# Attention with three slots a step instead of five, and the output projection gathered at the end of each round

## The chip, the cores and the metric

The kernel runs on one core of a Trainium2 chip. Its engines run side by side, each with its own queue of instructions in program order: TensorE (PE in the profile, its weight loads PEld), VectorE (DVE), ScalarE (ACT), GpSimd (POOL) and SyncE (SP), which issues most DMAs. They wait for one another on semaphores. TensorE writes its results into PSUM, eight banks of 128 partitions by 512 f32 numbers, from where VectorE and ScalarE read them. The metric is the device time of one execution in microseconds.

## What is computed

The program is a transformer block with two layers' parts: multi-query attention and a quantised feed-forward product, then a mixture of experts, a second attention and a second mixture of experts. The change is in the first attention alone: 2 batches, 1024 rows, 16 heads of 64 channels, one key and value head shared by all, a causal mask, and one extra "null" key.

```python
q = (xn @ Wq).reshape(b, n, H, DH).transpose(0, 2, 1, 3) * scale
k, v = (kv[..., :DH], kv[..., DH:])
...
sim = jnp.einsum('bhid,bjd->bhij', q, k)
sim = sim + bias
...
attn = jax.nn.softmax(sim, axis=-1)
out = jnp.einsum('bhij,bjd->bhid', attn, v)
out = out.transpose(0, 2, 1, 3).reshape(b, n, INNER)
out = out @ Wo
```

## The kernel before

The 1024 rows of a batch are 8 tiles of 128, and under the mask tile t sees t + 1 blocks of 128 keys. A **round** j, b pairs the long row tile 7 - j with the short row tile j of batch b, so that every round has 9 blocks. There are 8 rounds (j = 0 to 3, two batches each), and a round has 8 **steps**, one for each pair of heads; 64 steps in all. In the code unit 0 is the long row, unit 1 the short one.

A step's work comes in two streams. The **score stream** works for a later step: TensorE makes one of six chunks of scores (long row, head 0, two chunks; long row, head 1, two chunks; short row, one chunk a head; called s0 to s5 here), VectorE adds the bias, stores it in `probs` and keeps the minimum (L2265), ScalarE takes the exponential when a row and head is complete (L2200), VectorE inverts the sum (L2305), GpSimd multiplies the long row by it (L2154) and ScalarE the short one (L2210). Once a step TensorE also makes the queries of four steps later ("q", L2347), which ScalarE and VectorE split into a high and a low part (L2194, L2272). Chunks and queries share a **ring of two banks**, `s_ps`: item e goes to bank e % 2, and TensorE waits until item e - 2 has been read, by `wait(pe, s_read, e - 1)`. SyncE loads the bias and moves the queries.

The **value stream** works for the present step. It is cut into slots of up to two key blocks, five a step. `turn(n)` on TensorE transposes the probabilities of slot n into a bank `t_ps` (L2369), `high(n)` on ScalarE copies them rounded to `pT_hi` (L2182), `low(n)` on VectorE takes the rest to `pT_lo` (L2287), and `weigh(n)` on TensorE multiplies both parts with the values into `o_ps` (L2389, L2390). There are three `t_ps` banks. When a row ends, ScalarE copies the lower half of `o_ps` (L2187), VectorE adds the two halves into `oT` (L2300), and `project` multiplies it with `Wo` into the bank `y_ps`, which gathers the whole round (L2398). At the end of a round the null key's share is added (L2403), and ScalarE copies the result to `yacc` (L2216).

The order on each engine is written out by hand. Step x occupies slots 5x to 5x + 4, and the table `SCORES_AT` says at which slot a score chunk or query stands: of step x + 2 the chunks s0 and s1 in the first slot, then one chunk a slot, and the query in the third. At slot n TensorE does the first score item, a projection if a row ended three slots ago, `turn(n + 2)`, the other score items, `weigh(n)`. ScalarE does `high(n + 1)`, the copy of a row that ended, the query, the exponentials. VectorE does the first score item, `low(n + 1)`, the other items, the sum of a row that ended, the inversion.

## Time and profile before

| | |
|---|---|
| median of 3 runs | 1084.52 us (1079.64 to 1092.77) |
| span of the profiled execution | 1077.8 us |
| attention, from the first to the last transposition into `t_ps` | 60.8 to 610.1 us |
| busy over the span: TensorE, VectorE, ScalarE, GpSimd | 86%, 74%, 68%, 57% |
| granted TensorE clock in the attention, between 100 and 600 us | 1.00 |

The profile is of one execution on one core, taken by the hardware. Its own time is not in the table of runs; the span is from its first instruction to its last, 6.7 us below the median. A row of the timeline gives start and duration in us, then engine, line, operation, output and inputs, shape, and how many instructions were merged; in brackets the idle time before it and what ended that. Matmuls are pipelined, so a row's duration is longer than the distance to the next matmul: four transpositions have the duration 0.60 us and follow one another every 0.11 us.

### The profile page before, as it was taken

The page shows a single profiled execution, that of the slowest core. Times are in us where ns is not written, and L with a number is a line of the kernel's source. Part 1 is how long each engine was busy: PE and PEld are TensorE (multiplying, and loading weights), DVE is VectorE, ACT ScalarE, POOL GpSimd, SP SyncE. Part 2 cuts the span into 40 slices and gives each one's busy share as a digit, 9 for nine tenths or more (in the row PEclk, how much of TensorE's full clock was granted, in tenths as well). Part 3 has the DMA queues.
Part 4 walks back from the last instruction along what each step waited for, and adds up shares of the span by engine and source line. Part 5 has one row for each costly group of instructions (what it writes and reads, how often), then busy time and mean ns, then how long its engine had stood idle before and what let it go on. Part 6 is the DMA issues. An engine that isn't in the chain of part 4 may idle for free. (4 is left out here: it accounts for less than half of the span.)

```text
span 1077.8 us, 22664 instructions
## 1 busy us (share of the span) xinstructions
PE 930.0 (86%) x6178; PEld 811.2 (75%) x6178; DVE 799.7 (74%) x2315; ACT 735.9 (68%) x1651; POOL 610.6 (57%) x745
## 2 busy tenths in 40 slices
PE   7899999999999999999999849678753882499996
PEld 5578888888888998988888637568752662399995
DVE  7579989899898998988888798465458776244443
ACT  2278888888888998989989656235564552466663
POOL 2368878777676676755555364544572147244444
PEclk8889999999999999999999969799976885699998
DMA  9166666667566666665666031348926013444453
GB/s 308 38 184 182 177 179 181 177 175 199 156 189 198 179 190 179 192 205 165 192 175 199 28 133 42 115 147 270 320 86 196 21 69 133 107 77 78 76 82 45
DMA packets 110549, 162.83 MB, mean 151 GB/s; under 512 B 15993, under 2 KB 84089, under 8 KB 109402
## 3 DMA queue, kind: packets, MB, share of 16 engines
q1 hardware_dynamic: 99272, 142.16, 44.6%
q0 software_dynamic: 10560, 19.18, 7.8%
q8 instruction: 54, 0.88, 0.3%
q14 instruction: 69, 0.57, 0.2%
q10 hardware_dynamic: 594, 0.04, 0.0%
HBM read 110.63 MB, written 25.53 MB: 126 GB/s over the span
## 5 line engine op out<-in xcount | busy, mean ns | idle before, releaser
L2154 POOL TENSOR_SCALAR probs<-probs,inv_sum 128x1024 f32<-128x1024 f32 (+3 forms) x128 | 301.4, 2368 | 172.9 <-DVE inv_sum L2305 172.9
L2287 DVE TENSOR_TENSOR pT_lo<-t_ps,pT_hi 128x512 fp32r<-128x512 f32 (+1 forms) x320 | 202.8, 634 | 21.1 <-ACT pT_hi L2182 20.6
L2200 ACT ACTIVATE probs<-probs,neg_max 128x1025 f32<-128x1025 f32 (+7 forms) x256 | 197.6, 772 | 29.9 <-DVE neg_max L2265 28.6
L2369 PE MATMUL t_ps<-ident,probs 128*128 128x128 f32 x1152 | 180.3, 275 | 1.1 <-DVE pT_lo L2287 1.1
L2182 ACT ACTIVATE pT_hi<-t_ps 128x512 fp32r<-128x512 f32 (+1 forms) x320 | 175.3, 549 | 6.4 <-PE t_ps L2369 3.2
L2389 PE MATMUL o_ps<-pT_hi,values 128*128 128x256 f32 x576 | 174.8, 323 | 5.3 <-DVE pT_lo L2287 3.5
L2265 DVE CUSTOM_DVE_ANT_0 probs<-s_ps,bias_set,neg_null 128x512 f32<-128x512 f32 (+3 forms) x256 | 164.3, 642 | 4.5 <-PE s_ps L2338 2.8
L2369 PEld LDWEIGHTS t_ps<-ident,probs 128*128 128x128 f32 x1152 | 142.2, 141 | 31.3 <-DVE pT_lo L2287 3.1
L2390 PE MATMUL o_ps<-pT_lo,values 128*128 128x256 f32 x576 | 150.2, 280 | 0.0
L2337 PE MATMUL s_ps<-k_hi,q_hilo 128*128 128x512 f32 (+3 forms) x384 | 143.1, 373 | 4.7 <-DVE neg_max L2265 1.5
L2338 PE MATMUL s_ps<-k_lo,q_one 128*128 128x512 f32 (+3 forms) x384 | 134.4, 350 | 0.0
L2389 PEld LDWEIGHTS o_ps<-pT_hi,values 128*128 128x128 f32 x576 | 108.8, 189 | 16.8 <-issue 8.3
L1772 POOL DMA_INDIRECT out_dram<-yacc,xs x39 | 63.4, 1626 | 89.8 <-DVE yacc L1841 51.1
L2390 PEld LDWEIGHTS o_ps<-pT_lo,values 128*128 128x128 f32 x576 | 109.6, 190 | 0.0
L153 POOL DMA_INDIRECT routed_rows<-rt_rows,rt_rows_at x64 | 68.0, 1062 | 49.8 <-DVE rt_rows_at L198 31.3
L2337 PEld LDWEIGHTS s_ps<-k_hi,q_hilo 128*128 128x128 f32 x384 | 73.2, 191 | 16.6 <-DVE part_max L2265 10.1
L2398 PE MATMUL y_ps<-wo,oT 128*128 128x256 f32 x256 | 77.0, 382 | 0.5 <-DVE oT L2300 0.4
L2338 PEld LDWEIGHTS s_ps<-k_lo,q_one 128*128 128x128 f32 x384 | 73.6, 192 | 0.0
L2300 DVE TENSOR_TENSOR oT<-o_ps,o_low 64x128 f32<-64x128 f32 x256 | 71.4, 279 | 2.3 <-ACT o_low L2187 0.6
L1785 ACT ACTIVATE w_qkv<-m_x_ps,ln_b,ln_w 128x128 f32<-128x128 f32 x78 | 31.4, 454 | 59.7 <-PE m_x_ps L1855 59.7
L2265 DVE CUSTOM_DVE_ANT_0 probs<-s_ps,bias_set,part_max 128x512 f32<-128x512 f32 (+3 forms) x128 | 69.7, 545 | 1.5 <-PE s_ps L2338 1.3
L2347 PE MATMUL s_ps<-xs,wq_all 128*128 128x128 f32 x496 | 67.7, 280 | 2.9 <-DVE neg_max L2265 2.9
(348 smaller groups left out, 2135.3 us busy)
## 6 DMA issues: line engine op xcount, KB each, us to landing
bias_set<-bias_dram SPq DMA_DIRECT2D x16, 1024.0 KB, 5.4
bias_set<-bias_dram SPq DMA_DIRECT2D x16, 896.0 KB, 5.4
bias_set<-bias_dram SPq DMA_DIRECT2D x16, 768.0 KB, 4.9
bias_set<-bias_dram SPq DMA_DIRECT2D x16, 640.0 KB, 4.7
q_hilo<-q_hi SPq DMA_DIRECT2D x128, 64.0 KB, 2.0
q_hilo<-q_lo SPq DMA_DIRECT2D x128, 64.0 KB, 2.0
q_one<-q_hi SPq DMA_DIRECT2D x128, 64.0 KB, 2.0
bias_set<-bias_dram SPq DMA_DIRECT2D x16, 512.0 KB, 5.5
```

The costliest lines, as they stand in the source:

```text
L2154: last = pool.tensor_scalar(keys, keys, inv_sum[:, x.set, unit, h:h + 1], None, ALU.mult)
L2182: act.activation(pT_hi[n % 3][:, 0:count, :], t_ps[TURNS["slot", n] % 3][:, 0:2 * P * count], ACT.Copy).then_inc(hi_out, 1)
L2200: act.activation(p, p, ACT.Exp, scale=-1.0, bias=neg_max[:, x.set, row.unit, h:h + 1], accum_out=row_sum[:, x.set, row.unit, h:h + 1]).the ...
L2265: dve.tensor_tensor_reduce(probs_row(x, row, h)[:, 1 + P * first:1 + P * (first + count)], s_ps[e % 2][:, 0:P * count], bias_row(x, row, h ...
L2287: dve.tensor_tensor(pT_lo[n % 3][:, 0:count, :], t_ps[TURNS["slot", n] % 3][:, 0:2 * P * count].rearrange("p (n q) -> p n q", n=count), pT ...
L2300: last = dve.tensor_tensor(oT[row.unit][DH * h:DH * h + DH, :], o_ps[row.unit][0:DH, cols], o_low[row.unit][:, cols], ALU.add)
L2337: pe.matmul(s_ps[e % 2][:, 0:P * count], q_hilo[x.set][h][:, mine], k_hi[:, cols], start=True, stop=False)
L2338: pe.matmul(s_ps[e % 2][:, 0:P * count], q_one[x.set][h][:, mine], k_lo[:, cols], start=False, stop=True).then_inc(s_ready, 1)
L2369: last = pe.transpose(t_ps[at % 3][:, P * (2 * m + h):P * (2 * m + h) + P], probs_row(x, row, h)[:, 1 + P * (k + m):1 + P * (k + m) + P], ...
L2389: pe.matmul(o_ps[row.unit], v, pT_hi[n % 3][:, m, :], start=(k + m == 0), stop=False)
L2390: last = pe.matmul(o_ps[row.unit], v, pT_lo[n % 3][:, m, :], start=False, stop=(k + m == row.blocks - 1))
L2398: pe.matmul(y_ps[:, row.unit, :], oT[row.unit][:], wo[:, x.pair, :], start=first, stop=False, skip_group_check=True).then_inc(projected, 1)
```

## The change

Slots are up to four blocks instead of two, and a step has three: two for the long row (half of it each) and one for the short row. The two `t_ps` buffers are two PSUM banks each. The bank for them comes from `y_ps`, which goes. `oT` keeps the outputs of all eight pairs of a round, and the projection becomes an item of the score ring: at the round's end, for each of the two rows, eight products and the null key's one are made in a row into an `s_ps` bank ("y"), and ScalarE copies it. The transposed null weights go through the ring as well ("null").

The order by hand changes with it. Each slot has two chunks of scores: s2 and s3 in a step's first slot, s4 and s5 in its second, and s0 and s1 of the next step in its third. The query is third in the first slot in rounds j = 0 and 1, and third in the second slot in rounds j = 2 and 3. TensorE does `turn(n + 1)` (before: `turn(n + 2)`), then all score items of the slot, then `weigh(n)`.

```diff
-SLOTS_A_STEP = 5
+SLOTS_A_STEP = 3
...
-        self.slots = [(k, min(2, self.blocks - k)) for k in range(0, self.blocks, 2)]
+        half = self.blocks if unit else (self.blocks + 1) // 2
+        self.slots = [(k, min(half, self.blocks - k)) for k in range(0, self.blocks, half)]
...
-SCORES_AT = {n: [] for n in range(-1, NS)}
+SCORES_AT = {n: [] for n in range(-1, NS + 3)}
 for _x in range(STEPS):
-    for _i, _t in enumerate((0, 0, 1, 2, 3, 4)):
+    for _i, _t in enumerate((-1, -1, 0, 0, 1, 1)):
         SCORES_AT[max(-1, SLOTS_A_STEP * (_x - LEAD) + _t)].append(("s", _x, _i))
     if _x >= FIRST_Q:
-        SCORES_AT[max(-1, SLOTS_A_STEP * (_x - QLEAD) + 2)].append(("q", _x))
+        _at = SLOTS_A_STEP * (_x - QLEAD)
+        SCORES_AT[max(-1, _at + (ROUNDS[max(0, _x - QLEAD) // PAIRS][0] >= 2))].append(("q", _x))
+    if (_x + 1) % PAIRS == 0:
+        _r, _end = _x // PAIRS, SLOTS_A_STEP * (_x + 1)
+        SCORES_AT[_end - 1].append(("null", _r))
+        SCORES_AT[_end].append(("y", _r, 0))
+        SCORES_AT[_end + 1].append(("y", _r, 1))
 SCORES_AT[-1].sort(key=lambda item: (item[1] - (QLEAD - LEAD - 0.5 if item[0] == "q" else 0), item[0], item[2:]))
-RING = {item: i for i, item in enumerate(item for n in range(-1, NS) for item in SCORES_AT[n])}
+for _n in range(NS + 3):
+    SCORES_AT[_n].sort(key=lambda item: ("null", "s", "q", "y").index(item[0]))
+ORDER = [item for n in range(-1, NS + 3) for item in SCORES_AT[n]]
+RING = {item: i for i, item in enumerate(ORDER)}
...
-        self.pT_hi = [sbuf(st, f"pT_hi{i}", [P, 2, 2 * P], F32R) for i in range(3)]
-        self.pT_lo = [sbuf(st, f"pT_lo{i}", [P, 2, 2 * P], F32R) for i in range(3)]
-        self.oT = [sbuf(st, f"oT{i}", [P, P]) for i in range(2)]
+        self.pT_hi = [sbuf(st, f"pT_hi{i}", [P, 4, 2 * P], F32R) for i in range(2)]
+        self.pT_lo = [sbuf(st, f"pT_lo{i}", [P, 4, 2 * P], F32R) for i in range(2)]
+        self.oT = [sbuf(st, f"oT{i}", [P, PAIRS, P]) for i in range(2)]
...
-        t_ps = [psum(st, f"t_ps{i}", [P, CW]) for i in range(3)]
+        t_ps = [psum(st, f"t_ps{i}", [P, 4 * 2 * P]) for i in range(2)]
         o_ps = [psum(st, f"o_ps{i}", [P, CW])[:, 0:2 * P] for i in range(2)]
-        y_ps = psum(st, "y_ps", [P, 2, D])
...
-                    wait(act, pv_done, n - 2)
+                    wait(act, pv_done, n - 1)
                     act.wait_ge(turn_ready, n + 1)
-                    act.activation(pT_hi[n % 3][:, 0:count, :], t_ps[TURNS["slot", n] % 3][:, 0:2 * P * count], ACT.Copy).then_inc(hi_out, 1)
+                    act.activation(pT_hi[n % 2][:, 0:count, :], t_ps[n % 2][:, 0:2 * P * count], ACT.Copy).then_inc(hi_out, 1)
...
-                def result(r):
+                def result(r, unit):
                     j, b = ROUNDS[r]
-                    act.wait_ge(y_ready, r + 1)
-                    for unit, tile in enumerate((QT - 1 - j, j)):
-                        last = act.activation(yacc[:, QT * b + tile, :], y_ps[:, unit, :], ACT.Copy)
-                    last.then_inc(y_out, 1)
+                    e = RING["y", r, unit]
+                    act.wait_ge(s_ready, e + 1)
+                    apart(act, marks_act)
+                    act.wait_ge(s_read, e)
+                    act.activation(yacc[:, QT * b + (j if unit else QT - 1 - j), :], s_ps[e % 2][:, 0:D], ACT.Copy).then_inc(s_read, 1)
...
+                def null_weights(r):
+                    e = RING["null", r]
+                    dve.wait_ge(s_ready, e + 1)
+                    dve.tensor_copy(null_wT[r % 2][:], s_ps[e % 2][0:H, 0:2 * P]).then_inc(s_read, 1)
+
                 def fill(item):
+                    e = RING[item]
+                    if e and ORDER[e - 1][0] == "y":
+                        dve.wait_ge(s_read, e)
                     if item[0] == "q":
                         query(item[1])
-                    else:
+                    elif item[0] == "s":
                         scores(item[1], item[2])
+                    elif item[0] == "null":
+                        null_weights(item[1])
...
+                def project(r, unit):
+                    e = RING["y", r, unit]
+                    pe.wait_ge(oT_ready, units_done(PAIRS * r + PAIRS - 1, unit))
+                    pe.wait_ge(s_read, RING["null", r] + 1)
+                    wait(pe, s_read, e - 1)
+                    for pair in range(PAIRS):
+                        pe.matmul(s_ps[e % 2][:, 0:D], oT[unit][:, pair, :], wo[:, pair, :], start=(pair == 0), stop=False)
+                    pe.matmul(s_ps[e % 2][:, 0:D], null_wT[r % 2][:, P * unit:P * unit + P], null_wo[:],
+                              start=False, stop=True).then_inc(s_ready, 1)
...
-                def project(x, row):
-                    first = x.pair == 0 and row.unit == 0
-                    if first:
-                        wait(pe, y_out, x.round)
-                    pe.wait_ge(oT_ready, units_done(x.g, row.unit))
-                    pe.matmul(y_ps[:, row.unit, :], oT[row.unit][:], wo[:, x.pair, :],
-                              start=first, stop=False, skip_group_check=True).then_inc(projected, 1)
-                    if x.pair == PAIRS - 1 and row.unit == 1:
-                        pe.wait_ge(t_read, TURNS["null", x.round] + 1)
-                        for unit in range(2):
-                            last = pe.matmul(y_ps[:, unit, :], null_wT[x.round % 2][:, P * unit:P * unit + P], null_wo[:],
-                                             start=False, stop=True, skip_group_check=True)
-                        last.then_inc(y_ready, 1)
 
                 for item in SCORES_AT[-1]:
                     fill(item)
-                for n in range(2):
-                    turn(n)
-                for n in range(NS + 6):
-                    if n < NS:
-                        for item in SCORES_AT[n][:1]:
-                            fill(item)
-                    ended = ends_at(n - 3)
-                    if ended:
-                        project(*ended)
-                    if n < NS:
-                        turn(n + 2)
-                    if n < NS:
-                        for item in SCORES_AT[n][1:]:
-                            fill(item)
-                    if n < NS:
-                        weigh(n)
+                turn(0)
+                for n in range(NS + 3):
+                    turn(n + 1)
+                    for item in SCORES_AT[n]:
+                        fill(item)
+                    weigh(n)
```

On TensorE, in a step of a round with j = 1 (7 and 2 blocks), before: from the second product of s2 (128x512) over a projection, a turn, a `weigh` and s3 (128x384) to the query, which is the last row.

```order
L2338 MATMUL s_ps<-k_lo,q_one_1 128x512
L2398 MATMUL y_ps<-wo,oT 128x256
L2369 MATMUL t_ps<-ident,probs 128x128 x2
L2389 MATMUL o_ps<-pT_hi,values 128x256
L2390 MATMUL o_ps<-pT_lo,values 128x256
L2389 MATMUL o_ps<-pT_hi,values 128x256
L2390 MATMUL o_ps<-pT_lo,values 128x256
L2337 MATMUL s_ps<-k_hi,q_hilo_1 128x384
L2338 MATMUL s_ps<-k_lo,q_one_1 128x384
L2398 MATMUL y_ps<-wo,oT 128x256
L2369 MATMUL t_ps<-ident,probs 128x128 x4
L2347 MATMUL s_ps<-xs,wq_all 128x128 x4
```

After, the same place: s2, s3 and the query stand in a row.

```order
L2396 MATMUL t_ps<-ident,probs 128x128 x6
L2343 MATMUL s_ps<-k_hi,q_hilo_1 128x512
L2344 MATMUL s_ps<-k_lo,q_one_1 128x512
L2343 MATMUL s_ps<-k_hi,q_hilo_1 128x384
L2344 MATMUL s_ps<-k_lo,q_one_1 128x384
L2353 MATMUL s_ps<-xs,wq_all 128x128 x4
L2410 MATMUL o_ps<-pT_hi,values 128x256
L2411 MATMUL o_ps<-pT_lo,values 128x256
```

The query is two ring items behind s2 in both. Now only s3 stands between them, where before a projection, two turns and a `weigh` did as well.

On VectorE before the change, from the read of s2 to the query's split. `L2265` is the read of a score chunk, its second row the accumulator's.

```order
L2265 ISA probs,part_max<-s_ps,bias_set,neg_null 128x512
L2265 ISA part_max 128x1
L2287 TENSOR_TENSOR pT_lo<-t_ps,pT_hi 128x512
L2265 ISA probs,neg_max<-s_ps,bias_set,part_max 128x384
L2265 ISA neg_max 128x1
L2287 TENSOR_TENSOR pT_lo<-t_ps,pT_hi 128x256
L2272 SCALAR_TENSOR_TENSOR q_lo<-s_ps,q_hi 128x256
```

After, from the low part of a step's first slot (1024 columns) over the read of s2 (the second chunk of 128x512, part_max) to the query's split and what stands behind it:

```order
L2296 TENSOR_TENSOR pT_lo<-t_ps,pT_hi 128x1024
L2264 ISA probs,neg_max<-s_ps,bias_set,part_max 128x384
L2264 ISA neg_max 128x1
L2306 TENSOR_TENSOR oT<-o_ps,o_low 64x128 x2
L2311 RECIPROCAL inv_sum<-row_sum 128x2
L2264 ISA probs,part_max<-s_ps,bias_set,neg_null 128x512
L2264 ISA part_max 128x1
L2296 TENSOR_TENSOR pT_lo<-t_ps,pT_hi 128x768
L2264 ISA probs,neg_max<-s_ps,bias_set,part_max 128x384
L2264 ISA neg_max 128x1
L2271 SCALAR_TENSOR_TENSOR q_lo<-s_ps,q_hi 128x256
L2306 TENSOR_TENSOR oT<-o_ps,o_low 64x128 x2
```

The read of s2 now stands behind a low part of twice the columns, the read of s1, the long row's sum and an inversion.

On ScalarE, from the copy of a query to the high part of the next step's first slot (its last `pT_hi` row), in a round with j = 1, before:

```order
L2194 ACTIVATE q_hi<-s_ps 128x256
L2182 ACTIVATE pT_hi<-t_ps 128x512
L2200 ACTIVATE probs,row_sum<-probs,neg_max 128x897
L2182 ACTIVATE pT_hi<-t_ps 128x512
L2187 ACTIVATE o_low<-o_ps 64x256
```

And after:

```order
L2194 ACTIVATE q_hi<-s_ps 128x256
L2200 ACTIVATE probs,row_sum<-probs,neg_max 128x897
L2182 ACTIVATE pT_hi<-t_ps 128x512
L2200 ACTIVATE probs,row_sum<-probs,neg_max 128x897
L2210 ACTIVATE probs<-probs,inv_sum 128x256 x2
L2182 ACTIVATE pT_hi<-t_ps 128x1024
```

Two exponentials and the short row's two products with the inverse now lie between the query's copy and that high part, where one exponential did.

Behind a round's end on TensorE after the change (the first step of round 4, `SCORES_AT` slot 3 * 32 + 1): the projection of round 3's short row, between the slot's score items and its `weigh`.

```order
L2343 MATMUL s_ps1<-k_hi,q_hilo1_1 128x384
L2344 MATMUL s_ps1<-k_lo,q_one1_1 128x384
L2353 MATMUL s_ps0<-xs,wq_all 128x128 x4
L2372 MATMUL s_ps1<-wo,oT1 128x256 x8
L2373 MATMUL s_ps1<-null_wo,null_wT1 128x256
```

Before, these eight products were spread over the eight steps, one a step and row, as the first piece of this section shows.

## Rows read from the trace of the kernel before

**Rows 1.** The page: busy time, share of the span and instructions of each engine.

```profile
PE 930.0 (86%) x6178; PEld 811.2 (75%) x6178; DVE 799.7 (74%) x2315; ACT 735.9 (68%) x1651; POOL 610.6 (57%) x745
```

**Rows 2.** Windows: stretch, length, busy us of each engine, granted clock, DMA.

```profile
300.00:400.00 100.00, 98.88 (x714) 89.54 (x713) 91.36 (x284) 90.71 (x215) 70.23 (x96) 1.00 0.63 185
...
720.00:1078.00 358.00, 265.92 (x1741) 235.69 (x1739) 188.41 (x447) 185.76 (x385) 158.77 (x157) 0.85 0.47 122
```

**Rows 3.** Waits from 70 to 600 us: who for whom, total us, times, longest.

```profile
ACT q_hi L2194 <- PE s_ps L2347: 34.5, 47, 1.9
DVE q_lo L2272 <- ACT q_hi L2194: 23.3, 38, 1.8
...
PEld s_ps L2337 <- DVE part_max L2265: 7.8, 31, 0.3
```

**Rows 4.** Timeline, one step of round 2 (j = 1), TensorE.

```profile
302.02 0.19 PEld L2337 LDWEIGHTS s_ps<-k_hi,q_hilo 128*128 128x128 f32 x1 [0.24 <-DVE part_max L2265]
...
303.71 0.34 PE L2337 MATMUL s_ps<-k_hi,q_hilo 128*128 128x384 f32 x1
...
304.06 0.59 PE L2398 MATMUL y_ps<-wo,oT 128*128 128x256 f32 x2
...
304.49 0.60 PE L2369 MATMUL t_ps<-ident,probs 128*128 128x128 f32 x4
...
304.93 1.06 PE L2347 MATMUL s_ps<-xs,wq_all 128*128 128x128 f32 x8
...
305.74 0.36 PE L2389 MATMUL o_ps<-pT_hi,values 128*128 128x256 f32 x1
...
306.30 0.28 PE L2337 MATMUL s_ps<-k_hi,q_hilo 128*128 128x256 f32 x1
...
310.59 0.19 PEld L2337 LDWEIGHTS s_ps<-k_hi,q_hilo 128*128 128x128 f32 x1 [0.24 <-DVE part_max L2265]
```

**Rows 5.** Timeline, the same step, ScalarE.

```profile
302.33 0.60 ACT L2182 ACTIVATE pT_hi<-t_ps 128x512 fp32r<-128x512 f32 x1
...
303.20 1.05 ACT L2200 ACTIVATE probs<-probs,neg_max 128x897 f32<-128x897 f32 x1 [0.27 <-DVE neg_max L2265]
...
304.24 0.89 ACT L2210 ACTIVATE probs<-probs,inv_sum 128x256 f32<-128x256 f32 x2
...
305.04 0.36 ACT L2182 ACTIVATE pT_hi<-t_ps 128x256 fp32r<-128x256 f32 x1
...
306.08 0.39 ACT L2194 ACTIVATE q_hi<-s_ps 128x256 fp32r<-128x256 f32 x1 [0.68 <-PE s_ps L2347]
```

**Rows 6.** Timeline, the same step, VectorE.

```profile
303.02 0.57 DVE L2300 TENSOR_TENSOR oT<-o_ps,o_low 64x128 f32<-64x128 f32 x2
...
303.71 0.73 DVE L2265 CUSTOM_DVE_ANT_0 probs<-s_ps,bias_set,neg_null 128x512 f32<-128x512 f32 x1
...
304.37 0.69 DVE L2287 TENSOR_TENSOR pT_lo<-t_ps,pT_hi 128x512 fp32r<-128x512 f32 x1
...
304.97 0.61 DVE L2265 CUSTOM_DVE_ANT_0 probs<-s_ps,bias_set,part_max 128x384 f32<-128x384 f32 x1
...
305.50 0.42 DVE L2287 TENSOR_TENSOR pT_lo<-t_ps,pT_hi 128x256 fp32r<-128x256 f32 x1
...
306.50 0.42 DVE L2272 SCALAR_TENSOR_TENSOR q_lo<-s_ps,q_hi 128x256 fp32r<-128x256 f32 x1 [0.58 <-ACT q_hi L2194]
```

**Rows 7.** Timeline, VectorE: the same query split in five rounds, marks for a round's length.

```profile
138.90 0.42 DVE L2272 SCALAR_TENSOR_TENSOR q_lo<-s_ps,q_hi 128x256 fp32r<-128x256 f32 x1 [1.36 <-ACT q_hi L2194]
...
209.19 0.42 DVE L2272 SCALAR_TENSOR_TENSOR q_lo<-s_ps,q_hi 128x256 fp32r<-128x256 f32 x1 [1.79 <-ACT q_hi L2194]
...
351.41 0.42 DVE L2272 SCALAR_TENSOR_TENSOR q_lo<-s_ps,q_hi 128x256 fp32r<-128x256 f32 x1 [1.29 <-ACT q_hi L2194]
...
485.56 0.42 DVE L2272 SCALAR_TENSOR_TENSOR q_lo<-s_ps,q_hi 128x256 fp32r<-128x256 f32 x1 [1.09 <-ACT q_hi L2194]
...
555.99 0.42 DVE L2272 SCALAR_TENSOR_TENSOR q_lo<-s_ps,q_hi 128x256 fp32r<-128x256 f32 x1 [1.08 <-ACT q_hi L2194]
```

75 lines of the change are left out of this document (34 added, 41 removed).

## The prediction

> **What bounds the kernel now.** I read the page first, for the size of the part that changes. Then I read the windows of the attention, the table of waits, and the timeline of one step. The page [rows 1] has TensorE at 86% of the span and VectorE at 74%. That is a mean over stages, and the change touches only the attention, some 550 of 1078 us. In a window inside it [rows 2] TensorE is busy 98.9 of 100 us, and VectorE and ScalarE 91 each, at a granted clock of 1.00. By that view TensorE is the limit. The timeline says less than that: the busy rows overlap. The distances between rows are the work: transpositions 0.11 us each (four from 304.49 to 304.93), a query (304.93 to 305.74) and a chunk of 384 columns 0.35 us (303.71 to 304.06), so one of 512 is 0.47 and one of 256 (a little over the share) 0.24, a projection product 0.43 (304.06 to 304.49), a weighing product 0.12 (four in the 0.56 us from 305.74 to 306.30, with some wait in front) [rows 4]. The query's eight instructions take 0.92 at that spacing. A step has 18 transpositions, 18 weighing products, six chunks, a query and two projection products: 2.0 + 2.1 + 2.1 + 0.9 + 0.9 = 8.0 us. The step itself takes 302.02 to 310.59, 8.57 us [rows 4], so TensorE is at 93%, and the missing 0.6 us is in the waits.
>
> The waits name a loop over three engines [rows 3]: ScalarE waits for the query (34.5 us in all), VectorE for ScalarE's copy of it (23.3 us), TensorE for VectorE's read of a chunk, in order to get its ring bank back (7.8 us). It can be followed through one step: the bank is free at 302.02, TensorE works until the query, ScalarE copies it at 306.08, VectorE splits it at 306.50 and then works without a gap through s4, a low part, s5, a low part, the sum and s0, whose end frees the bank at 310.59 [rows 4 to 6]. So the period is 4.06 us on TensorE and its hand-over, 0.42 us on ScalarE and 4.09 us on VectorE. The kernel is held by this loop, not by an engine's load, and the question for the change is what its loop will be.
>
> **The change: what it removes.** Slots fall from 320 to 192, so 128 copies on ScalarE and 128 subtractions on VectorE go. A copy of 512 columns takes 0.60 us and one of 256 takes 0.36 [rows 5], so 0.12 of it is fixed; a subtraction takes 0.69 and 0.42 [rows 6], fixed 0.15. Two a step are 0.24 us on ScalarE and 0.30 on VectorE, 15 and 19 us over 64 steps if either were the limit. A copy of 1024 columns should be 1.08 us and a subtraction 1.23 (both worked out from those two rows; no instruction over two banks is in the trace, and I keep 0.1 us either way). TensorE's work stays at 8.0 us a step in the mean. GpSimd, SyncE and the DMAs keep their order per step and have slack (GpSimd busy 70 of 100 us [rows 2]); I cost them at nothing, and their inputs come no later against their use.
>
> **What it adds: a longer loop.** In rounds j = 0 and 1 the query is third in its slot, behind s2 and s3, and needs the bank of s2. Before, TensorE came to it long after that read. Now only s3 is between. VectorE reads s2 behind the low part of the first slot, s1, the sum and the inversion. That low part needs ScalarE's high part, and ScalarE does that behind the query's copy, two exponentials and the short row's products. So for j = 1, from the end of one read of s2:
> TensorE takes up the query in 0.2 us (an estimate, from the hand-over at 302.02), and ScalarE starts its copy 1.15 us later (304.93 to 306.08) [rows 4, 5]: 1.35.
> ScalarE in a row: the query 0.39, exponential 1.04 (303.20 to 304.24), high part of two blocks 0.60, exponential 1.04, short row's products 0.80 (304.24 to 305.04), high part of four blocks 1.08 [rows 5]: 4.95, or 4.85 since successive starts lie closer.
> VectorE in a row: low part of four blocks 1.15 (start to start), read of s1 0.53 (304.97 to 305.50), sum 0.60 (before 303.71), inversion 0.1, read of s2 0.73 [rows 6]: 3.1.
> Together 9.3 us, against 8.57. The side paths are shorter: TensorE goes from the query through weigh, turn, s4, s5, weigh and turn to s0 in 4.8 us and is early by 0.4 us. The same additions for the other rounds (exponentials and reads scaled by their columns) give 9.15 us for j = 0. For j = 2 and 3, where the query is third in the second slot and needs the bank of s4, two low parts and both sums are on the way, and they give 9.6 and 9.4.
>
> **What it adds: the projection in a row.** Eight products and the null key's are nine times 0.43, 3.9 us, in each of two neighbouring slots. Queued behind them on TensorE is weigh, and behind that the turn and the chunks for which ScalarE and VectorE wait. Their queues hold some 1 to 2 us of work by then and then run dry. The first product also waits for the read of the chunk two before it, 0.2 to 0.6 us. In the loop above, both lie between the query and the next high part, so I add them nearly whole: 4.35 + 4.3 us for j = 1, after taking off the 0.4 us that TensorE is early; 9.1, 8.6, 8.0 and 8.8 us for j = 0 to 3. The bounds are 2 us (all but the excess over the other engines' queues hidden) and 9 us. I take the upper part, for the nearest case in the trace: two j = 1 rounds take 351.41 - 209.19 = 142.2 us [rows 7], 71.1 each, and eight steps of 8.57 are 68.6. The null products, their copy and the two result copies, some 1 us of TensorE, cost 2.5 us of time. What stands at a round's end is not hidden in this pipeline. The null copy now comes ahead of the low part and s0: 0.7 us a round.
>
> **The sum.** Round lengths before are 70.3 us (j = 0), 71.1, 67.1 (half of 485.56 - 351.41) and 70.4 (j = 3) [rows 7]; they hold the projection and the round's end. After: 8 x 9.15 + 9.1 = 82.3, 8 x 9.3 + 8.6 = 83.0, 8 x 9.6 + 8.0 = 84.8, 8 x 9.4 + 8.8 = 84.0. The differences are 12.0, 11.9, 17.7 and 13.6 us, twice each: 110 us. The null copies add 5. The last two steps have no scores, and the last projection of the long row hides in part: less 5. That is 110 us on a profiled span of 1077.8, and the same on the median: 1084.5 + 110 = **1195 us**, 10% slower.
>
> The Trainium skill ("Perfetto Trace Analysis", Matmul Optimizations) says that it is important that matmuls run back to back in batches, because the engine's power follows its use. That speaks for the gathered projection; but the granted clock is 1.00 here already [rows 2], so by this trace the batch has nothing to win. The same page (Matmuls) wants independent groups to rotate through banks, so that the reading of one overlaps the next: three groups in a row on a ring of two do less of that.
>
> **The rivals.**
> *Faster: the ring holds nobody.* If VectorE comes to s2 before TensorE comes to the query, the engines' loads decide. TensorE's 8.0 us a step against 8.57 saves 0.57 x 64 = 36 us, and the exposed last projection gives 4 back: 1052 us. For it: fewer instructions, fewer waits. It decides once ScalarE's chain from the query to the high part is 3.5 us instead of 4.85 (9.3 less 1.3 is TensorE's 8.0); above 4.1 us the steps are slower than before. Against it: the orders as printed, and rows 5. 7%.
> *One half only.* The steps lengthen (for j = 0 to 3 by 0.6, 0.7, 1.6 and 0.9 us, 16 steps each) and the batches hide: 61 us, 1145. Or the batches cost and the steps stay as they are: 110 less 61 is 49 us, 1134. For them: both are walks through queues, and a queue that runs ahead further than I let it hides one or the other. 20%.
> *The clock falls.* TensorE will wait some 2 us in each step and more around the batches. In the last third of the program, where it is busy 266 of 358 us, its granted clock is 0.85 [rows 2]. At 0.85 the query and the batches in the loop, 2.2 us a step, are 18% longer: 25 us more, 1220; if its side chain becomes the longer one, 1240. The Trainium skill ("TensorE: Matmul & The Clock Gate", What's actually happening) has throttled as the default, which activity releases. 12%.
> *No change*, gains and losses of the same size: 5%.
> The forecast itself has 56%.
>
> **How the numbers follow.** The likeliest case is 1195. To hold 8 in 10, the range goes down to the half cases, 1135 and up to the clock's, 1235. Within 1% is about what a measurement of this kernel can't tell from no change. Faster by more than that 0.07, within it 0.05, slower 0.88.
>
> **What would show it.** In the profile after: the same query splits 9.1 to 9.6 us apart in a round's middle; TensorE's idle time or long first matmul in front of the query, released by VectorE's read; ScalarE without a gap from q_hi to the copy of 1024 columns; a row of 16 or 18 projection matmuls of 3.9 us, with VectorE idle behind it; rounds of 82 to 85 us. It is wrong if the query doesn't wait for VectorE, if ScalarE's or VectorE's two-bank instructions are much shorter than by the slopes, or if VectorE stays busy through a projection.

## The result, and the profile after

The changed kernel takes 1231.39 us (median of 4 runs, 1228.48 to 1236.10), the kernel before 1084.47 us beside it: a ratio of 1.1343 [1.1291, 1.1394], 147 us more. The profiled execution has a span of 1226.7 us and a mean granted clock of 0.910 (before 1077.8 us and 0.921). The forecast was 1195 us in a range of 1135 to 1235.

The page of the changed kernel: the span, the busy time of each engine (before in [rows 1]), the granted clock in 40 slices, and two groups of the attention.

```profile
span 1226.7 us, 22188 instructions
...
PE 982.4 (80%) x6178; PEld 833.6 (68%) x6178; DVE 794.8 (65%) x2187; ACT 723.8 (59%) x1523; POOL 614.8 (50%) x745
...
PEclk8899999988988999999999999697899598589999
...
L2182 ACT ACTIVATE pT_hi<-t_ps 128x768 fp32r<-128x768 f32 (+3 forms) x192 | 155.1, 808 | 38.4 <-PE t_ps L2396 35.6
...
L2194 ACT ACTIVATE q_hi<-s_ps 128x256 fp32r<-128x256 f32 x62 | 23.9, 385 | 123.9 <-PE s_ps L2353 123.9
```

The removed instructions are gone (128 fewer on VectorE, 128 fewer on ScalarE), and both engines are busy for less time than before. Neither was the limit. ScalarE now idles 123.9 us in front of the 62 copies of a query: two microseconds in each step.

The windows of the changed kernel, columns as in [rows 2]: one in j = 1, one in j = 3.

```profile
300.00:400.00 100.00, 84.78 (x519) 74.31 (x518) 66.32 (x192) 63.69 (x141) 55.40 (x72) 0.90 0.49 141
500.00:600.00 100.00, 85.47 (x541) 69.33 (x540) 69.80 (x199) 67.52 (x145) 48.66 (x73) 1.00 0.48 141
```

TensorE fell from 98.9 busy us of 100 to 85, and VectorE and ScalarE from 91 to between 64 and 70. The first window also shows a granted clock of 0.90, where it was 1.00 before. In both windows no engine is full; that is a loop's picture, and the waits name it (70 to 700 us, columns as in [rows 3]).

```profile
DVE probs L2264 <- PE s_ps L2344: 132.7, 82, 7.0
ACT q_hi L2194 <- PE s_ps L2353: 116.9, 57, 2.8
PEld s_ps L2343 <- DVE neg_max L2264: 68.5, 71, 1.4
PEld s_ps L2353 <- DVE part_max L2264: 32.5, 31, 1.1
```

The last row is the wait of the forecast: TensorE holds the query back until VectorE has read s2. ScalarE waited 34.5 us for the query before [rows 3], now 116.9. The first row has the round's end in it: 7.0 us at the longest, for a chunk that stands behind a projection.

A step of the changed kernel in j = 0, as a timeline of TensorE, ScalarE and VectorE.

```profile
182.62 1.16 PE L2353 MATMUL s_ps<-xs,wq_all 128*128 128x128 f32 x8 [0.61 <-DVE part_max L2264]
...
183.88 0.39 ACT L2194 ACTIVATE q_hi<-s_ps 128x256 fp32r<-128x256 f32 x1 [2.23 <-PE s_ps L2353]
184.16 1.14 ACT L2200 ACTIVATE probs<-probs,neg_max 128x1025 f32<-128x1025 f32 x1
185.29 0.37 ACT L2182 ACTIVATE pT_hi<-t_ps 128x256 fp32r<-128x256 f32 x1
185.56 1.15 ACT L2200 ACTIVATE probs<-probs,neg_max 128x1025 f32<-128x1025 f32 x1
186.69 0.69 ACT L2210 ACTIVATE probs<-probs,inv_sum 128x128 f32<-128x128 f32 x2
187.32 1.03 ACT L2182 ACTIVATE pT_hi<-t_ps 128x1024 fp32r<-128x1024 f32 x1
...
187.99 0.75 DVE L2264 CUSTOM_DVE_ANT_0 probs<-s_ps,bias_set,neg_null 128x512 f32<-128x512 f32 x1 [1.00 <-PE s_ps L2344]
188.67 1.22 DVE L2296 TENSOR_TENSOR pT_lo<-t_ps,pT_hi 128x1024 fp32r<-128x1024 f32 x1
189.81 0.74 DVE L2264 CUSTOM_DVE_ANT_0 probs<-s_ps,bias_set,part_max 128x512 f32<-128x512 f32 x1
...
191.96 1.16 PE L2353 MATMUL s_ps<-xs,wq_all 128*128 128x128 f32 x8 [0.61 <-DVE part_max L2264]
```

From query to query it is 191.96 - 182.62 = 9.34 us. ScalarE goes from the query's copy to the copy of 1024 columns without a gap. Here a second branch of the loop is as long: VectorE idles 1.00 us until TensorE has s0 ready at 187.99, and only then comes to the low part. ScalarE's copy of 1024 columns is done at 188.35 (187.32 + 1.03), the low part starts at 188.67: by these rows it is s0, and not ScalarE's chain, that makes the step 9.33 where the walk had 9.15. The two-bank instructions take 1.03 and 1.22 us, against 1.08 and 1.23 by the slopes.

The batch of the long row behind the last round of j = 2 (it stands in the first step of j = 3), in the same three engines:

```profile
589.10 3.69 PE L2372 MATMUL s_ps<-wo,oT 128*128 128x256 f32 x16 [1.00 <-DVE part_max L2264]
592.72 0.69 PE L2373 MATMUL s_ps<-null_wo,null_wT 16*128 16x256 f32 x2
593.35 0.38 PE L2410 MATMUL o_ps<-pT_hi,values 128*128 128x256 f32 x1
...
593.54 0.39 ACT L2218 ACTIVATE yacc<-s_ps 128x256 f32<-128x256 f32 x1 [4.51 <-PE s_ps L2373]
595.29 1.03 ACT L2182 ACTIVATE pT_hi<-t_ps 128x1024 fp32r<-128x1024 f32 x1 [1.37 <-PE t_ps L2396]
...
595.85 0.75 DVE L2264 CUSTOM_DVE_ANT_0 probs<-s_ps,bias_set,neg_null 128x512 f32<-128x512 f32 x1 [5.53 <-PE s_ps L2344]
```

The batch waits 1.00 us for a bank and then holds TensorE 4.25 us (589.10 to 593.35). ScalarE is idle for 4.51 us until the batch itself is ready to be copied and for 1.37 more until the next turn; VectorE works on for 1.2 us into the batch and is then idle for 5.53, until a chunk that is queued behind it.

The marks of a round's length, as in [rows 7]:

```profile
165.64 0.42 DVE L2271 SCALAR_TENSOR_TENSOR q_lo<-s_ps,q_hi 128x256 fp32r<-128x256 f32 x1
...
254.12 0.42 DVE L2271 SCALAR_TENSOR_TENSOR q_lo<-s_ps,q_hi 128x256 fp32r<-128x256 f32 x1 [0.84 <-ACT q_hi L2194]
...
346.69 0.42 DVE L2271 SCALAR_TENSOR_TENSOR q_lo<-s_ps,q_hi 128x256 fp32r<-128x256 f32 x1 [1.04 <-ACT q_hi L2194]
...
425.87 0.42 DVE L2271 SCALAR_TENSOR_TENSOR q_lo<-s_ps,q_hi 128x256 fp32r<-128x256 f32 x1 [0.32 <-ACT q_hi L2194]
...
511.97 0.42 DVE L2271 SCALAR_TENSOR_TENSOR q_lo<-s_ps,q_hi 128x256 fp32r<-128x256 f32 x1 [0.32 <-ACT q_hi L2194]
```

Rounds are 88.5, 92.6 and 86.1 us (254.12 - 165.64, 346.69 - 254.12, 511.97 - 425.87), where 82 to 85 were forecast. Between the same splits in a round's middle it is 9.33 us for j = 0, 9.48 for j = 2 and 9.51 for j = 3. For j = 1, and in the last two steps of j = 0 before its batches (11.25 and 10.95), they are uneven: some 9.3 to 9.5, others 10.0 to 11.5 us. A window over one of the long ones shows a low clock, and its query is slow:

```profile
273.70:284.90 11.20, 9.64 (x58) 8.80 (x58) 7.55 (x22) 7.31 (x17) 6.36 (x8) 0.80 0.54 150
...
282.68 1.72 PE L2353 MATMUL s_ps<-xs,wq_all 128*128 128x128 f32 x8 [0.73 <-DVE part_max L2264]
```

A query of 1.16 us takes 1.72 here. So there are three parts to explain: longer steps, longer round's ends, and a clock that falls, for the most part in j = 1.

### The profile page after: what moved, and what is told of

Read it like the earlier page. It is cut to its first block and busy times, and to the rows that moved or that the text cites. A ratio compares the mean times of both kernels' runs of the same rounds, so it can differ in the third digit from the quotient of the medians.

```text
span 1226.7 us, 22188 instructions
## 1 busy us (share of the span) xinstructions
PE 982.4 (80%) x6178; PEld 833.6 (68%) x6178; DVE 794.8 (65%) x2187; ACT 723.8 (59%) x1523; POOL 614.8 (50%) x745
## 5 line engine op out<-in xcount | busy, mean ns | idle before, releaser
L2343 PE MATMUL s_ps<-k_hi,q_hilo 128*128 128x512 f32 (+3 forms) x384 | 158.3, 416 | 52.4 <-DVE neg_max L2264 42.4
L2296 DVE TENSOR_TENSOR pT_lo<-t_ps,pT_hi 128x768 fp32r<-128x768 f32 (+3 forms) x192 | 183.3, 955 | 21.9 <-ACT pT_hi L2182 21.5
L2182 ACT ACTIVATE pT_hi<-t_ps 128x768 fp32r<-128x768 f32 (+3 forms) x192 | 155.1, 808 | 38.4 <-PE t_ps L2396 35.6
L2410 PE MATMUL o_ps<-pT_hi,values 128*128 128x256 f32 x576 | 164.8, 313 | 5.9 <-DVE pT_lo L2296 3.8
L2396 PE MATMUL t_ps<-ident,probs 128*128 128x128 f32 x1152 | 161.0, 277 | 0.0
L2396 PEld LDWEIGHTS t_ps<-ident,probs 128*128 128x128 f32 x1152 | 134.7, 144 | 0.3 <-issue 0.2
L2353 PE MATMUL s_ps<-xs,wq_all 128*128 128x128 f32 x496 | 78.5, 306 | 41.6 <-DVE part_max L2264 23.7
L2353 PEld LDWEIGHTS s_ps<-xs,wq_all 128*128 128x128 f32 x496 | 65.3, 205 | 64.0 <-DVE part_max L2264 35.3
L2194 ACT ACTIVATE q_hi<-s_ps 128x256 fp32r<-128x256 f32 x62 | 23.9, 385 | 123.9 <-PE s_ps L2353 123.9
L2142 POOL COPY probs<-neg_null 128x2 f32<-128x2 f32 x128 | 19.6, 189 | 116.2 <-PE t_ps L2396 104.9
```

Source lines behind the costliest of these rows:

```text
L2182: act.activation(pT_hi[n % 2][:, 0:count, :], t_ps[n % 2][:, 0:2 * P * count], ACT.Copy).then_inc(hi_out, 1)
L2296: dve.tensor_tensor(pT_lo[n % 2][:, 0:count, :], t_ps[n % 2][:, 0:2 * P * count].rearrange("p (n q) -> p n q", n=count), pT_hi[n % 2][:, 0 ...
L2343: pe.matmul(s_ps[e % 2][:, 0:P * count], q_hilo[x.set][h][:, mine], k_hi[:, cols], start=True, stop=False)
L2353: last = pe.matmul(s_ps[e % 2][:, P * row.unit:P * row.unit + P], wq_all[:, c, 2 * x.pair:2 * x.pair + 2, :], xnT[:, c, P * t:P * t + P], ...
L2396: last = pe.transpose(t_ps[n % 2][:, P * (2 * m + h):P * (2 * m + h) + P], probs_row(x, row, h)[:, 1 + P * (k + m):1 + P * (k + m) + P], i ...
L2410: pe.matmul(o_ps[row.unit], v, pT_hi[n % 2][:, m, :], start=(k + m == 0), stop=False)
```

## The experiments

Four experiments ran on the chip that has 1084 us for the kernel before: the gathered projection alone, the one product, the query first, and the extra products. The others ran on two chips that took 1053 and 1054 us for it. So each kernel is compared by its ratio to the kernel before on its own chip, with its 95% interval. By the traces the 30 us lie behind the attention: from the last query split to the end it is 496 to 508 us on the first chip and 466 to 478 on the others, while changed kernels have the same steps of 9.33, 9.48 and 9.51 us on both. So a difference in us from the kernel before is told beside the ratio where it matters (125 us more there would be 129 by the ratio times 1084). The letters A and B in an expectation are the theories of that run. My overall theory was the forecast's two mechanisms; the rivals were that the slots' size makes the steps long, that the exposed projections are most of it, and that the clock is more than a small part.

**The gathered projection alone.** Five slots, the ring and `t_ps` as before; the eight pairs' outputs are kept and projected into `y_ps` at the round's end.

```diff
-                    first = x.pair == 0 and row.unit == 0
+                    if x.pair < PAIRS - 1:
+                        return
...
-                    pe.matmul(y_ps[:, row.unit, :], oT[row.unit][:], wo[:, x.pair, :],
-                              start=first, stop=False, skip_group_check=True).then_inc(projected, 1)
+                    for pair in range(PAIRS):
+                        last = pe.matmul(y_ps[:, row.unit, :], oT[row.unit][:, pair, :], wo[:, pair, :],
+                                         start=(pair == 0 and row.unit == 0), stop=False, skip_group_check=True)
+                    last.then_inc(projected, 1)
```

> The kernel before (five slots, three t_ps banks, y_ps) with only one part of the change: oT keeps all eight pairs and the sixteen products are made at the round's end, eight for each row, into y_ps. Theory A (the batches cost in themselves): a round's steps lose their two projection products of 0.43 us and fall to about 7.9 us, the round's end grows by the 6.9 us of products on TensorE, which nothing hides; round about 72 to 73 us against 70, in all 15 to 30 us slower, 1100 to 1115 us. Rival B (the other engines' queues carry them over a batch): 1084 us or less, since the steps are shorter.

1120.5 us, ratio 1.0331 [1.0286, 1.0375]. At the end of the first round the step in which both batches fall is 15.8 us long and its neighbours 8.9 and 8.8: 8.9 us more than three steps of 8.20. The timeline of such a step, at the end of the last round of j = 1:

```profile
361.56 3.62 PE L2402 MATMUL y_ps<-wo,oT 128*128 128x256 f32 x16
...
365.10 1.13 PE L2408 MATMUL y_ps<-null_wo,null_wT 16*128 16x256 f32 x4
...
368.00 0.42 DVE L2272 SCALAR_TENSOR_TENSOR q_lo<-s_ps,q_hi 128x256 fp32r<-128x256 f32 x1 [5.01 <-ACT q_hi L2194]
```

VectorE idles 5.01 us behind the batch. Mid-round steps of j = 0 and 1 fell by 0.3 us (8.50 to 8.20, 8.58 to 8.26), which fits with the 0.43 us product that stood ahead of the query; those of j = 2 and 3 stayed at 8.02 and 8.53. So the spread projection had cost some 10 us (0.3 in 32 steps), and gathering it costs by itself 3.3%, in the kernel of five slots too. That is 36 us where theory A had 15 to 30: it had the steps fall to 7.9, and in j = 2 and 3 they did not fall at all.

**The batch without seven of its eight products** (changed kernel).

```diff
-                    for pair in range(PAIRS):
+                    for pair in range(1):
                         pe.matmul(s_ps[e % 2][:, 0:D], ...
```

> The changed kernel with one of the eight pairs' products in each batch instead of eight (it leaves out seven eighths of the output projection; the null key's product stays). Theory A (a batch is exposed whole): 14 x 8 products of 0.43 us less, 48 us, so 1183 us, a little less if the clock recovers with it. Rival B (batches mostly hidden, the steps carry the loss): 1210 us or more. The steps in a round's middle stay at 9.3 to 9.5 us under both.

1178.2 us, ratio 1.0898 [1.085, 1.0946]: 53 us less by the medians, 52 by the spans, 48 by the ratios (0.0445 x 1084). The 7 x 16 products at 0.45 us (3.62 us for eight, the row above) are 50 us. They are exposed nearly whole, as expected: by the splits a round is 6.05 us shorter in j = 0 and 2, for 14 products less. Mid-round steps stay at 9.33, 9.48 and 9.51 us, and the low clock of j = 1 stays (0.91 between 200 and 400 us). So the steps don't owe their length to the batches.

**The query's place in the changed kernel.** First in its slot:

```diff
-    SCORES_AT[_n].sort(key=lambda item: ("null", "s", "q", "y").index(item[0]))
+    SCORES_AT[_n].sort(key=lambda item: ("null", "q", "s", "y").index(item[0]))
```

> The changed kernel with the query as the first score item of its slot instead of the last, so that it needs the bank of the chunk read a slot earlier. Theory A (the steps are held by the loop read of s2 or s4, query, ScalarE, low part): the query no longer waits for that read and the steps get shorter, by my walk only to about 9.1 us for j = 0 and 1, as ScalarE's copy of the query and the chunk behind it close a loop nearly as long, and to about 8.8 for j = 2 and 3: 1205 to 1215 us. Rival B (the steps are held by the two-bank buffers of the value stream, turn to weigh): no change, 1231.

1202.18 us, ratio 1.1113 [1.1072, 1.1155]. Steps of 9.77, 9.14, 8.85 and 9.09 us for j = 0 to 3: shorter by 0.1 to 0.6 where the loop through s2 or s4 was (9.21 for j = 1 with the clock kept up, see below), longer in j = 0, where 9.1 was expected. The time is a little under the 1205 to 1215 of theory A. The steps alone are 16 x (0.07 + 0.63 + 0.42 - 0.44) = 11 us of the 29; the rest fits with the clock, which stayed at 1.00 in j = 1:

```profile
300.00:400.00 100.00, 86.28 (x583) 74.20 (x583) 75.49 (x216) 72.58 (x157) 60.43 (x80) 1.00 0.52 152
```

And between the two chunks:

```diff
+    _kinds = [item[0] for item in SCORES_AT[_n]]
+    if _kinds[:3] == ["s", "s", "q"]:
+        SCORES_AT[_n].insert(1, SCORES_AT[_n].pop(2))
```

> The changed kernel with the query second in its slot, between the two chunks: it then needs the bank of the chunk before (s1 or s3), read earlier on VectorE by a sum, an inversion and a read. Theory A (the loop through the query's bank): its length falls by up to 1.4 us; by a walk through the queues about 8.7 us a step for j = 0 and 1, and 8.6 to 8.9 for j = 2 and 3, where it was 9.3 to 9.5 (11.2 at the lower clock): 1165 to 1185 us. The batches at the rounds' ends stay, 10 us each. Rival B: 1200 us or more, no better than the query first.

1146.39 us, ratio 1.0893 [1.0843, 1.0944]: a third of the loss is back, 93 us over the kernel before and not 147. A window over one step of j = 2 shows TensorE busy 8.16 of 8.60 us again, and the query splits of j = 1 follow one another at 8.73 us:

```profile
503.40:512.00 8.60, 8.16 (x58) 6.95 (x57) 7.52 (x23) 7.52 (x17) 5.66 (x8) 1.00 0.59 180
...
278.39 0.41 DVE L2274 SCALAR_TENSOR_TENSOR q_lo<-s_ps,q_hi 128x256 fp32r<-128x256 f32 x1
...
287.12 0.41 DVE L2274 SCALAR_TENSOR_TENSOR q_lo<-s_ps,q_hi 128x256 fp32r<-128x256 f32 x1
```

The steps are 9.49, 8.73, 8.60 and 8.40 us. With the same slots, the same two-bank instructions and the same batches, moving the query by one place gives 0.5, 0.9 and 1.1 us a step back in j = 1, 2 and 3 (against 9.21, 9.48 and 9.51). Those are 37 us with the 0.16 that j = 0 loses, and the other 17 fit with the clock, 1.00 between 200 and 500 us here. In j = 0 nothing comes back; there VectorE waits for s0, as in the timeline of the changed kernel:

```profile
113.73 0.75 DVE L2267 CUSTOM_DVE_ANT_0 probs<-s_ps,bias_set,neg_null 128x512 f32<-128x512 f32 x1 [1.58 <-PE s_ps L2347]
```

Over before's 8.50, 8.58, 8.02 and 8.53, the steps cost 16 x (0.99 + 0.15 + 0.58 - 0.13) = 25 us, and the rest, 68 us, is what the rounds' ends cost.

**The query's place in the kernel before.** Five slots and no batch, but s2, s3 and the query together in the second slot, so that the query needs the bank of s2 as in the changed kernel:

```diff
-    for _i, _t in enumerate((0, 0, 1, 2, 3, 4)):
+    for _i, _t in enumerate((0, 0, 1, 1, 3, 4)):
...
-        SCORES_AT[max(-1, SLOTS_A_STEP * (_x - QLEAD) + 2)].append(("q", _x))
+        SCORES_AT[max(-1, SLOTS_A_STEP * (_x - QLEAD) + 1)].append(("q", _x))
```

> The kernel before (five slots of two blocks, three t_ps banks, projections spread) with its query and its chunk s3 both moved into the second slot, so that the query stands directly behind s2 and s3 as in the changed kernel. Nothing else is changed. Theory A (the steps of the changed kernel are long because the query is third in its slot, whatever the size of the slots): the loop goes from the read of s2 over the query and, on ScalarE, two exponentials, the short row's products and three high parts, 4.7 us, to the next step's first low part, and on VectorE over the sums and two low parts back to s2: about 10 us a step in place of 8.5, 1150 to 1190 us. Rival B (the bigger slots and the two instead of three buffers make the steps long): at most 1095 us.

1195.14 us, ratio 1.134 [1.1287, 1.1392], 142 us over the kernel before: as slow as the whole change, without any of its large slots or batches, and above what theory A had given. In its timeline ScalarE idles 3.44 us before each query:

```profile
285.57 0.39 ACT L2194 ACTIVATE q_hi<-s_ps 128x256 fp32r<-128x256 f32 x1 [3.44 <-PE s_ps L2347]
...
295.27 1.16 PE L2347 MATMUL s_ps<-xs,wq_all 128*128 128x128 f32 x8 [0.73 <-DVE part_max L2265]
...
296.52 0.38 ACT L2194 ACTIVATE q_hi<-s_ps 128x256 fp32r<-128x256 f32 x1 [3.44 <-PE s_ps L2347]
```

The steps are 10.67, 10.95, 10.94 and 11.34 us, a microsecond over what I had expected; which hand-over makes up that microsecond was not followed. So the query's place is enough to make the steps long, and the run before this one shows that with the large slots they are nearly as short as before in j = 1 to 3. The rival that large slots as such make the steps long falls for these rounds. For the 0.8 to 1.0 us of j = 0 it stays open: no run took apart the size of the slots, the two `t_ps` buffers and s0's place there.

One slot earlier and one slot later than before, nothing else (offset 2 becomes 1, or 3):

```diff
-        SCORES_AT[max(-1, SLOTS_A_STEP * (_x - QLEAD) + 2)].append(("q", _x))
+        SCORES_AT[max(-1, SLOTS_A_STEP * (_x - QLEAD) + 1)].append(("q", _x))
```

> The kernel before with one change: the query one slot earlier, behind s2 and ahead of s3 (it needs the bank of s1). In the kernel before the steps with j = 0, 1 and 3 are held at 8.5 to 8.6 us by the loop through s2, s3 and the query on TensorE, and TensorE's own work is 8.0. Theory A (that loop): s3's products and a projection leave its TensorE part, 0.8 us; steps fall to 8.0 to 8.3, 1060 to 1075 us. Rival B (ScalarE's row of query, exponential and the short row's products in that slot becomes the longer loop): 1085 us or more.

> The kernel before with one change: the query one slot later, behind s4. Theory A (the loop read of s0, s2, s3, query, ScalarE's copy, VectorE's split and the rest): the query needs the bank of s3 and the next step's s0 its own, and the split stands behind s4 and its low part, so ScalarE's copy is not waited for any more; steps of 8.0 to 8.4 us, 1060 to 1080. Rival B (the query then delays s5 and the next step's s0): 1085 us or more.

1096.01 us, ratio 1.04 [1.0346, 1.0454], and 1092.22 us, ratio 1.0359 [1.031, 1.0409]. Both times my theory A fell and the rival held. The waits of the first and of the second, 70 to 600 us:

```profile
ACT q_hi L2194 <- PE s_ps L2347: 96.5, 56, 2.2
DVE pT_lo L2287 <- ACT pT_hi L2182: 57.8, 57, 1.5
```

```profile
ACT q_hi L2194 <- PE s_ps L2347: 81.4, 57, 2.3
...
PEld o_ps L2389 <- DVE oT L2300: 26.1, 32, 0.8
```

ScalarE's wait for the query grows from 34.5 us [rows 3] to 96.5 and 81.4, over the same 530 us. The second rows were 17.0 us (VectorE for ScalarE's copy) and 5.3 (TensorE for the sum) before. As a last variant TensorE does the query directly behind the slot's first chunk, ahead of the projection and the turn:

```diff
+                    ahead = 2 if n < NS and len(SCORES_AT[n]) > 1 and SCORES_AT[n][1][0] == "q" else 1
...
-                        for item in SCORES_AT[n][:1]:
+                        for item in SCORES_AT[n][:ahead]:
```

> The kernel before with one change of order on TensorE alone: in a step's third slot the query stands directly behind s3, ahead of the projection and the turn that stood between them. The loop that holds the steps with j = 0, 1 and 3 at 8.5 to 8.6 us loses these 0.87 us on TensorE; then the bank of s2, read at 304.44, admits the query 0.3 us earlier than now. Theory A: 8.2 to 8.3 us in those rounds, 8.0 in j = 2 as before, 12 to 18 us faster, ratio 0.985 to 0.99. Rival B (the turn that is now later is missed by ScalarE's high part): ratio 1.00 or more.

1076.02 us, ratio 1.0219 [1.0201, 1.0238]: slower as well, where theory A had 0.985 to 0.99. ScalarE's wait for the query shrinks from 34.5 to 9.7 us (70 to 600 us), but the turn and s4 behind it are late, and VectorE now waits 47.0 us for chunks and ScalarE 18.3 for turns:

```profile
301.40 0.48 DVE L2265 CUSTOM_DVE_ANT_0 probs<-s_ps,bias_set,neg_null 128x256 f32<-128x256 f32 x1 [0.83 <-PE s_ps L2338]
...
307.40 1.16 PE L2347 MATMUL s_ps<-xs,wq_all 128*128 128x128 f32 x8 [0.27 <-DVE part_max L2265]
...
309.52 0.60 ACT L2182 ACTIVATE pT_hi<-t_ps 128x512 fp32r<-128x512 f32 x1 [0.49 <-PE t_ps L2369]
```

So the loop that I had read in the kernel before was one of several of nearly the same length; which of them holds each of the three variants was not followed. Of the places tried, the kernel's own is the best; no version of this study is faster than the kernel before.

**The clock.** Three more first products of chunk s3, whose result the real one overwrites, stand on TensorE ahead of the query in j = 0 and 1, where it waits anyway:

```diff
+                    for _ in range(3 if i == 3 and x.round < 4 else 0):
+                        pe.matmul(s_ps[e % 2][:, 0:P * count], q_hilo[x.set][h][:, mine], k_hi[:, cols], start=True, stop=True)
```

> The changed kernel with three more, useless first products of chunk s3 (rounds j = 0 and 1 only), some 0.5 us of TensorE work a step in time that TensorE waits for the query's bank. Theory A (the steps of 11.2 us with j = 1 are the lower clock, which falls because TensorE idles before the query): granted clock back to about 1.00 between 200 and 400 us, all those steps at 9.3 us, 20 us faster, 1210. Rival B (the 11.2 us steps have another cause, or the clock falls from the idle time at a batch): steps of 11.2 stay or get longer, 1231 to 1240.

1213.82 us, ratio 1.1184 [1.1135, 1.1232]: with work added, 17.6 us are gained. In windows and timeline:

```profile
300.00:400.00 100.00, 88.23 (x599) 77.42 (x598) 71.95 (x211) 70.99 (x155) 57.96 (x76) 0.98 0.52 150
...
282.11 0.42 DVE L2271 SCALAR_TENSOR_TENSOR q_lo<-s_ps,q_hi 128x256 fp32r<-128x256 f32 x1 [0.32 <-ACT q_hi L2194]
291.32 0.42 DVE L2271 SCALAR_TENSOR_TENSOR q_lo<-s_ps,q_hi 128x256 fp32r<-128x256 f32 x1 [0.32 <-ACT q_hi L2194]
```

The granted clock goes from 0.90 to 0.98, and the steps of j = 1 are 9.21 us, each like the other. So the loop's own length there is 9.21, and what stands above it was the clock. Which idle time pulls it down isn't shown. It isn't the share of it alone: the tight query in the kernel before leaves TensorE less busy, in the same rounds, and the clock stays at 1.00:

```profile
300.00:400.00 100.00, 81.63 (x553) 69.77 (x551) 72.30 (x221) 68.06 (x167) 58.43 (x73) 1.00 0.51 144
```

**The round's end in the changed kernel.** The batch behind `weigh` instead of ahead of it:

```diff
                     for item in SCORES_AT[n]:
-                        fill(item)
+                        if item[0] != "y":
+                            fill(item)
                     weigh(n)
+                    for item in SCORES_AT[n]:
+                        if item[0] == "y":
+                            fill(item)
```

> The changed kernel with each batch of projection products placed behind its slot's weighing products instead of ahead of them. Theory A (the other engines run dry because the next slot's turn and chunks are queued behind the batch): those stay behind it, so nothing is won but the earlier end of weigh: ratio to before within 0.5% of the changed kernel's 1.134. Rival B (it is weigh, and with it the copy of a finished row, that is missed): 15 us or more faster, ratio 1.12 or less.

1186.75 us, ratio 1.1285 [1.1249, 1.1322]. The round's ends are 1.4 us shorter by the splits (18.07 and 14.46 us for the steps of the batches in j = 0 and 2, where they were 19.52 and 15.21), which makes 11 us for eight rounds. The intervals of the two ratios overlap, and by differences it is 133 us against 147, a part of it the clock of j = 1 (0.95 and 0.92 in two windows of 100 us, against 0.91 and 0.90). So the gain is small: moving the batches by one item hides little of their 8.5 us a round.

Without the transposed null weights, their copy and their products (the null key's share of the result is missing):

```diff
-        SCORES_AT[_end - 1].append(("null", _r))
...
-                    pe.matmul(s_ps[e % 2][:, 0:D], null_wT[r % 2][:, P * unit:P * unit + P], null_wo[:],
-                              start=False, stop=True).then_inc(s_ready, 1)
```

> The changed kernel without the null key's item in the ring: the transposition of the null weights, its copy on VectorE and the null product at the end of each batch are left out (the null key's share of the output is missing). Theory A (a round's end costs more than I forecast because of what stands with the products: a third item in the ring of two at the last slot, and the null product's own wait, 0.6 us where 0.43 was counted): 2 to 3.5 us a round, 16 to 28 us faster, ratio 1.11 to 1.12. Rival B (the excess is in the products alone): at most 8 us, ratio 1.127 or more.

1178.63 us, ratio 1.1191 [1.117, 1.1213]: by the ratios 0.0152 x 1084 = 16 us, by the differences from the kernel before 147 - 125 = 22. The splits stand between: rounds are 2.35 us (j = 0), 2.64 (j = 2) and 2.3 (j = 3) shorter, some 19 us in all.

## Why the prediction was right or wrong

The direction and the two mechanisms were right; the size was 37 us short (110 forecast, 147 measured). That 1231 is still inside the range is in part luck: its upper end, 1235, was set for the clock alone, and the clock and longer round's ends both came. By its terms:

**The longer loop: right, 61 us forecast, 63 measured.** Steps were forecast at 9.15, 9.3, 9.6 and 9.4 us and are 9.33, 9.21 (with the clock kept up), 9.48 and 9.51. Less the 8.50, 8.58, 8.02 and 8.53 of before, 16 steps each, that is 13 + 10 + 23 + 16 us. In j = 0 TensorE's side branch to s0, which the walk had as early by 0.4 us for j = 1, was the longer one by 0.2. That the query's place makes the steps long is shown twice for j = 1 to 3: the tight query in the kernel before is as slow as the change, and the query between the two chunks leaves 25 of the 63 us. Of these 16 are in j = 0, where the query's place is not what holds the step.

**The gathered projection: exposed, as said, but 49 us (54 with the null copies) were too few.** This is the term that was mis-sized most, "so I add them nearly whole: 4.35 + 4.3 us for j = 1". A round's end, as the round's length less eight of its steps, is now 10.9 us for j = 0 and 1 (j = 0 in its first round, 85.53 us from the split at 80.11 to that at 165.64, since the second has slow steps; j = 1 in the run with the filled clock: 84.6 - 8 x 9.21), 10.3 for j = 2 and 12.3 for j = 3; the forecast had 9.1, 8.6, 8.0 and 8.8. Before it was 2.3, 2.5, 2.9 and 2.2 us by the same reckoning. The difference of those is 69 us over eight rounds. Some 1.5 us of the 12.3 are the clock: the step with that batch takes 17.17 us at 0.90, the one a round earlier 15.67 at 1.00. A batch takes 4.25 us and not 3.87: eight products 3.62 and the null key's 0.63. It also waits 0.5 to 1.0 us for its bank, where I had 0.2 to 0.6, and had taken off 0.4 for TensorE being early. And the null item costs: without it and its products 16 to 22 us go, where the sum had 5 for the copy and 7 for the products at 0.43. By the splits the run with one product takes away 48 us and the run without the null key 19. If the two add, that is the 69 us or nearly; both in one kernel were not tried. Of the 1 to 2 us of work that I had in the other engines' queues, VectorE had 1.2 at the batch shown above and ScalarE none (its idle time starts at 589.03).

**The clock: left to a rival at 12%, and it came, for 18 us.** The forecast held it at 1.00 in the attention. That was right but for the last two steps of j = 0 (0.86 from 212 to 235 us), j = 1 (0.90 in the mean) and one batch in j = 3. The rival had the mechanism but gave it every round, at 25 us. The Trainium skill ("TensorE: Matmul & The Clock Gate", What's actually happening) has throttled as the default, released by activity; the filled waits of this case agree (0.90 to 0.98 with some 0.5 us more work a step, an estimate by the 0.17 us between a chunk's products). The tight query in the kernel before does not fit with less activity alone: 81.6 of 100 us busy, at 1.00. What sets j = 1 of the changed kernel apart from that, and from the window of 500 to 600 us with TensorE busy 85.5 of 100 against 84.8, stays open.

**The removed instructions** saved nothing, as reckoned: VectorE is 4.9 us less busy and ScalarE 12.1, and both idle more. **The other rivals**: "the ring holds nobody" and "no change" fell; and of "one half only" both halves came.

Steps 63, round's ends 69 and clock 18 make 150, against 147 by the medians and 149 by the spans. Behind the last query split the changed kernel takes 10.8 us more (506.8 against 496.0), about what three longer steps and the last batches make by these terms; the less 5 of the sum for the program's end does not show.

The advice of the Trainium skill ("Perfetto Trace Analysis", Matmul Optimizations) to run matmuls back to back in batches was weighed against the granted clock in the prediction. The gathered projection alone took 3.3% here: the batch is dense on TensorE, and the engines that live on TensorE's output starve beside it.

## What to carry to other kernels

In a ring of two buffers, look at what item e - 2 is before moving item e: the wait it brings is for the reader of that item, and everything which that reader does first joins the loop. Two items moved so that the query came up behind s2 and s3 cost the kernel before as much as this whole change does. Work that was spread in small pieces over many steps may be nearly free there (some 10 us here); gathered, it costs its whole length as soon as the other engines' inputs are queued behind it, so count that as exposed unless a row shows work that covers it. And when a change makes TensorE wait in every step, price the clock too: it fell in the changed kernel (0.90 in a window with 84.8 us busy of 100) and not in that with the tight query (1.00 with 81.6). Some extra products into a bank that is overwritten are a cheap test.
